# A two-layer vision tower on one core: expert outputs stored from ScalarE's queue and read back by tiles, and the last window's values made early

## What is computed

```python
# layer 0, experts: 64 experts n, each fed one weighted mean of the tokens of an image
d = softmax(logits, axis=tokens); c = softmax(logits, axis=experts)
xs = einsum('bmd,bmn->bnd', xn, d)
h  = gelu(einsum('bnd,ndh->bnh', xs, w1) + b1)
ys = einsum('bnh,nhd->bnd', h, w2) + b2
y  = einsum('bnd,bmn->bmd', ys, c)              # back to the tokens: "combine"
# layer 1, attention over a 5 x 5 window of the (image, token) grid, 4 heads of 24
xs = gelu(x @ fc1 + convB(convA(x @ fc1)))
q, k, v = split(xs @ qkv_w.T + qkv_b)
out = softmax(q . k[window] + bias) @ v[window]
x + (out @ proj_w.T + proj_b) @ fc2_w.T + fc2_b
```

## Time and profile before

| | us |
|---|---|
| median of 3 runs | 970.0 (961.99 to 974.12) |
| the profiled execution | 967.93 |
| its span, first to last instruction | 965.4 |
| expert loop, PE's first to last product | 266.1 to 440.7 |
| combine products | 461.7 to 478.2 |
| neighbourhood attention, with its preparation | 478.7 to 671.0 |

### The profile page before, as it was taken

The page is one execution under the profiler, slowest core; times in us unless marked ns, Lnnn a source line. Parts: engine busy times, 40 slices in busy tenths (PEclk is TensorE's granted clock), DMA queues, the critical chain, the costliest instruction groups (busy, mean ns, idle before and its releaser), DMA issues.

```text
span 965.4 us, 17426 instructions
## 1 busy us (share of the span) xinstructions
PE 839.8 (87%) x6089; PEld 601.3 (62%) x6089; DVE 443.0 (46%) x1486; ACT 317.8 (33%) x906; POOL 306.0 (32%) x267
## 2 busy tenths in 40 slices
PE   6889999899999999884898899994357999999991
PEld 6778888676556665543864577773344666666661
DVE  5764655558633322222635478863871222222220
ACT  2543333226533332223033377762001212122110
POOL 1440000000000000000125254541947588888444
PEclk9999999999989999997899599996556999999996
DMA  8994000090059999995130000000224355544222
GB/s 249 259 297 187 1 2 1 1 391 2 2 204 422 421 420 421 421 380 147 43 137 0 1 2 1 0 2 1 57 78 116 81 106 105 105 93 103 39 25 24
DMA packets 59881, 129.03 MB, mean 134 GB/s; under 512 B 26334, under 2 KB 42256, under 8 KB 50112
## 3 DMA queue, kind: packets, MB, share of 16 engines
q1 hardware_dynamic: 29858, 118.72, 34.2%
q0 software_dynamic: 29952, 9.36, 7.1%
HBM read 115.87 MB, written 11.49 MB: 132 GB/s over the span
## 4 chain that ended last, share of the span: by engine, by line
PE 72%; DMA 12%; DVE 5%; issue 4%; ACT 2%; SPq 2%; POOL 2%; DVEq 0%; POOLq 0%; ACTq 0%
PE bank L1929 9%; PE bank L1943 6%; PE bank L1934 5%; PE bank L1213 4%; DMA w1l<-in_w_dram 4%; PE bank L1611 3%; DMA xT<-in_xT_dram 3%; PE bank L1187 3%; PE bank L849 3%; PE bank L877 3%; DMA w1s<-in_w_dram 2%; PE bank L810 2%; PE bank L1637 2%; PE bank L1191 2%; PE bank L857 2%
## 5 line engine op out<-in xcount | busy, mean ns | idle before, releaser
L1305 POOL MEMSET xg<- 96x74 f32 x1 | 0.2, 158 | 405.9 <-PE bank L1269 405.9
L1865 POOL DMA_INDIRECT out_dram<-yr,put x48 | 105.8, 2203 | 58.2 <-issue 46.8
L1929 PE MATMUL bank<-zTa,w 128*128 128x372 f32 x256 | 90.3, 497 | 0.8 <-DVE zTb L2003 0.8
L2012 DVE TENSOR_TENSOR hT<-sg,bank 128x372 f32<-128x372 f32 x64 | 31.8, 538 | 107.7 <-ACT sg L1973 66.3
L1852 POOL DMA_INDIRECT zr<-z_rows,take x48 | 66.7, 1389 | 27.1 <-issue 26.8
L1929 PEld LDWEIGHTS bank<-zTa,w 128*128 128x128 f32 x256 | 47.5, 194 | 38.2 <-ACT sg L1973 8.4
L1153 DVE COPY eh<-bank 128x384 f32<-128x384 f32 x32 | 17.9, 558 | 111.5 <-PE bank L1191 111.5
L1943 PE MATMUL bank<-w2r,hT 128*124 128x192 f32 x384 | 66.1, 329 | 0.8 <-DVE hT L2012 0.8
L1973 ACT ACTIVATE sg<-bank 128x372 f32<-128x372 f32 x64 | 27.3, 478 | 115.6 <-PE bank L1934 115.6
L1943 PEld LDWEIGHTS bank<-w2r,hT 128*124 128x124 f32 x384 | 61.9, 187 | 3.9 <-issue 3.9
L1346 POOL TENSOR_TENSOR nl<-nl,nr 111x1036 f32<-111x1036 f32 x22 | 42.1, 1914 | 60.3 <-DVE nr L1463 60.3
(11 more groups left out here) (311 smaller groups left out, 1757.8 us busy)
## 6 DMA issues: line engine op xcount, KB each, us to landing
w1l<-in_w_dram SPq DMA_DIRECT2D x20, 1152.0 KB, 16.0
w2l<-in_w_dram SPq DMA_DIRECT2D x20, 1152.0 KB, 16.8
w1s<-in_w_dram SPq DMA_DIRECT2D x12, 1152.0 KB, 14.9
w2s<-in_w_dram SPq DMA_DIRECT2D x12, 1152.0 KB, 15.0
w<-in_w_dram SPq DMA_DIRECT2D x8, 1024.0 KB, 7.8
xt<-in_x_dram SPq DMA_DIRECT2D x22, 336.0 KB, 8.9
xT<-in_xT_dram SPq DMA_DIRECT2D x22, 333.0 KB, 8.1
w2r<-in_w2r_dram SPq DMA_DIRECT2D x8, 384.0 KB, 4.0
```

What stands on the lines that cost most here:

```text
L1865: nc.gpsimd.indirect_dma_start(rows_out, bass.IndirectOffsetOnAxis(ap=put[:, k:k + 1], axis=0), yr[e % 2][:, j, :], None, bounds_check=OUT ...
L1929: nc.tensor.matmul(bank[to + 2 * part + half][:, 0:HS], w13[b][:, 0, at:at + 128], zTa[b][:, half * HS:(half + 1) * HS], start=True, stop= ...
L2012: nc.vector.tensor_tensor(hT[:, m, half * HS:(half + 1) * HS], sg[half][:], bank[4 * (m % 2) + 2 + half][:, 0:HS], ALU.mult).then_inc(s_hT, 1)
```

## The change

There are two parts. First, all 32 pairs are stored to `ys`, by ACT: right behind its copy to `eo` it waits for that copy and issues the two stores on its own DMA queue. SP's loop only loads. When all stores have landed, SP reads everything back in four spans of images (0 to 5, 6 to 10, 11 to 15, 16 to 21), each with one read into all 128 partitions of `e1` and one into 64 of `e2`; `product(t)` waits for the span that holds t. Second, the three value tiles of the last window move to the first three turns of the attention loop, each with two of the unread products behind it.

```diff
@@ experts_sp
+            for s in range(NPAIR):
...
-                p = s - RING
-                if p >= 0:
-                    sp.wait_ge(s_do, p + 1)
-                    for e in range(2):
-                        n = p + e * NPAIR
-                        if p < DIRECT:
-                            sp.dma_start(ys_of[n], eo[b][e * B:(e + 1) * B]).then_inc(s_eoo[b], 16)
-                        else:
-                            for to, lo, hi in places(n):
-                                sp.dma_start(to, eo[b][e * B + lo:e * B + hi]).then_inc(s_eoo[b], 16)
...
+            sp.wait_ge(s_dy, FREED + 1)
+            sp.dma_start(e2[NE:2 * NE, 0:T], ins["b2"].rearrange("n (t d) -> n t d", d=ED)).then_inc(s_el, 16)
+            for b in range(EOB):
+                sp.wait_ge(s_eoo[b], rows_out_by(NPAIR - EOB + b))
+            pairs = ys_of[:, 0:2 * (T - 1)].rearrange("n (g t) d -> g n t d", g=2)
+            for k, (lo, hi) in enumerate(SPANS):
+                sp.dma_start(e1[:, lo:hi], pairs[:, :, lo:hi]).then_inc(s_rows[k], 16)
+                last = T if hi == T - 1 else hi
+                sp.dma_start(e2[0:NE, lo:last], ys_of[:, 2 * (T - 1) + lo:2 * (T - 1) + last]).then_inc(s_rows[k], 16)
@@ experts_act, output(p)
                 nc.scalar.copy(eo[p % EOB][:], bank[6 + b][:, 0:ED]).then_inc(s_do, 1)
+                act.wait_ge(s_do, p + 1)
+                for e in range(2):
+                    act.dma_start(ys_of[p + e * NPAIR], eo[p % EOB][e * B:(e + 1) * B]).then_inc(s_eoo[p % EOB], 16)
@@ combine_pe
-            pe.wait_ge(s_el, 16 * (1 + 2 * GB))
-            for b in range(EOB):
-                pe.wait_ge(s_eoo[b], rows_out_by(NPAIR - EOB + b))
+            pe.wait_ge(s_el, 16)
...
             def product(t):
+                k = [lo <= t < hi or t == hi == T - 1 for lo, hi in SPANS].index(True)
+                pe.wait_ge(s_rows[k], rows_in(k))
@@ value_tiles
-            if isinstance(t, int):
-                return [T + 1, T + 2, T + 3] if t == T - 1 else [t + 2]
-            return [t + 2]
+            return [] if isinstance(t, int) and t == T - 1 else [t + 5]
@@ near_pool
-            for j in range(2):
+            for j in range(5):
                 source(j)
@@ near_dve, spread(t)
-                if after(t, 3):
-                    dve.wait_ge(s_fV, t)
+                dve.wait_ge(s_fV, t + 3)
@@ near_pe, query(t)
-                if after(t, 4):
-                    pe.wait_ge(s_fVc, t - 1)
-                elif t == 0:
-                    pe.wait_ge(s_fVc, 2)
+                pe.wait_ge(s_fVc, t + 2)
...
+                if isinstance(t, int) and t < 3:
+                    value(t + 2, t % 2)
+                    dense_near(2)
```

More of the change, by code:

```diff
@@ L34 @@
 EOB = 4
-DIRECT = 27
+FREED = 27
+SPANS = ((0, 6), (6, 11), (11, 16), (16, 21))
 HALF_HID = HID // 2
@@ L453, in tower @@
         s_cxc = sem("expert_input_stored")
-        s_w1 = [sem(f"w1_in{q}") for q in range(RING)]
-        s_w2 = [sem(f"w2_in{q}") for q in range(RING)]
+        s_w1 = [sem(f"w1_slot_in{q}") for q in range(RING)]
+        s_w2 = [sem(f"w2_slot_in{q}") for q in range(RING)]
+        s_rows = [s_w1[2], s_w2[2], s_w1[3], s_w2[3]]
         s_dh = sem("expert_hidden_product")
@@ L1065, in dispatch_pe, with rows_in @@
             over_tiles(pe, [(1, logits), (0, transpose_x), (4, inputs), (3, transpose_d)], T, unroll=8)
+        def rows_in(k):
+            return 16 * len(range(2 + k // 2, NPAIR, RING)) + 32
         def experts_sp(sp):
-            for s in range(NPAIR + RING):
+            for s in range(NPAIR):
                 q = s % RING
[L1072 to L1080, removed]
-                p = s - RING
-                if p >= 0:
-                    b = p % EOB
-                    sp.wait_ge(s_do, p + 1)
-                    for e in range(2):
-                        n = p + e * NPAIR
-                        if p < DIRECT:
-                            sp.dma_start(ys_of[n], eo[b][e * B:(e + 1) * B]).then_inc(s_eoo[b], 16)
-                        else:
-                            for to, lo, hi in places(n):
-                                sp.dma_start(to, eo[b][e * B + lo:e * B + hi]).then_inc(s_eoo[b], 16)
[L1092 to L1102, removed]
@@ L1104, in places @@
-        def places(n):
-            return ((e1[n:n + 1, 0:T - 1], 0, T - 1), (e1[NE + n:NE + n + 1, 0:T - 1], T - 1, 2 * (T - 1)), (e2[n:n + 1, 0:T], 2 * (T - 1), B))
+                if s == EARLY:
+                    sp.wait_ge(s_h, 2 * T)
+                if s >= RING:
+                    sp.wait_ge(s_dh, s - RING + 1)
+                sp.dma_start(w1s[q][:], ins["w1"][s]).then_inc(s_w1[q], 16)
+                if s >= RING:
+                    sp.wait_ge(s_dy, s - RING + 1)
+                sp.dma_start(w2s[q][:], ins["w2"][s]).then_inc(s_w2[q], 16)
@@ L1107, in rows_out_by @@
         def rows_out_by(p):
-            return sum(16 * (2 if r < DIRECT else 2 * GB) for r in range(p % EOB, p + 1, EOB))
+            return 32 * (p // EOB + 1)
         def experts_act(act):
@@ L1275, in value_columns @@
         def value_columns(j):
-            return j * TP if not isinstance(j, int) or j <= T else (B - WIN + PADR) * S + (j - T - 1) * TP
+            if isinstance(j, int) and j < 2:
+                return j * TP
+            if isinstance(j, int) and j < 5:
+                return (B - WIN + PADR) * S + (j - 2) * TP
+            return (j - 3) * TP
         def value_tiles(t):
-            if isinstance(t, int):
-                return [T + 1, T + 2, T + 3] if t == T - 1 else [t + 2]
-            return [t + 2]
+            return [] if isinstance(t, int) and t == T - 1 else [t + 5]
         def router_columns(c):
@@ L1337, in sources @@
             def sources(t, q):
-                source.b = q % 2
+                source.b = (q + 1) % 2
                 for j in value_tiles(t):
@@ L1435, in values, with last_values @@
                     dve.wait_ge(s_nA, t - 1)
-                for i, j in enumerate(value_tiles(t)):
-                    value(j, vl[i] if isinstance(t, int) and t == T - 1 else vn[(q + 2) % 4])
+                for j in value_tiles(t):
+                    value(j, vn[(q + 2) % 4])
+            def last_values(t, q):
+                if isinstance(t, int) and t < 3:
+                    value(t + 2, vl[t])
             for j in range(2):
@@ L1479, in residual @@
                 nc.vector.bn_stats(hst[:, t, :], h[:, t, :]).then_inc(s_hst, 1)
-            over_tiles(dve, [(4, copy_w), (2, reciprocal), (1, logits), (3, values), (0, spread), (5, residual)], T, unroll=4, tail=2)
+            over_tiles(dve, [(4, copy_w), (2, reciprocal), (1, logits), (3, values), (0, spread), (0, last_values), (5, residual)], T, unroll=4, tail=2)
         def near_act2(act):
@@ L1599, in values @@
                 for j in value_tiles(t):
-                    value(j, (j if isinstance(j, int) else q) % 2)
+                    value(j, (q + 1) % 2)
             for j in range(2):
@@ L1629, in values_out @@
                 tiles = vl if isinstance(t, int) and t == T - 1 else [vn[(q + i) % 4] for i in range(3)]
-                pe.wait_ge(s_fVc, VT if isinstance(t, int) and t == T - 1 else t + 3)
+                pe.wait_ge(s_fVc, VT if isinstance(t, int) and t == T - 1 else t + 6)
                 if after(t, 1):
```

## The result

The changed kernel takes 983.15 us (977.39 to 985.98, four runs) where before took 966.88 (961.99 to 974.12) in the same comparison: a ratio of 1.0162, 95% interval 1.0118 to 1.0206. The forecast was 982, from +11.9 us on the profiled execution; measured are +15.2 us between the two profiled executions (967.93 and 983.08) and +16.3 between the medians. That 982 is nearer to 983.15 than 11.9 is to 16.3 is luck: it comes from the median of before, 970.0 in the three runs shown then and 966.9 here.

The account below looks back on a forecast made before the run. The prediction saw the late way of the outputs into e1 and e2 as bounding the experts' end, 21 us before the combine. Terms +19.3, +2 and -9.4 on 967.93 gave 979.8, median 2.1 higher: 982 us, range 960 to 1000.

Parts of the forecast that it names:

- The number of engines: Read into e1: outermost counts 2 and 128 allow only two DMA engines, so the e1 data take 41.3 us.
- Their rate: Read into e1: each of the two engines moves 25 GB/s, with 18.4 as the other end.
- rival (b): Read-back: each of the two engines moves less, 18.4 GB/s, giving 998 us; chance 0.12.
- The read-back: Between experts and combine: the last span lands near 491.5 and the combine ends near 497.5, +19.3 us.
- the waits between the groups: Combine: products come in four groups with PE waits of about 10 us, each ended by a read.
- Stores on ACT: Expert loop: two stores per pair on ACT, 0.6 us each, stay hidden in 3.35 us free per pair.
- Rival (c): Expert loop: ACT is held by its issues at 3 us each, giving 1009 us; chance 0.04.
- The values at the start: First three attention turns: an added value and two unread products each cost +2 us, between -2 and +6.
- two of 1.49 / 6: First three attention turns: two unread products, at twice the time, take 0.5 us each; 5.0 us in all with the values.
- At the end: Attention loop's end: last values_out starts 7.0 us earlier, 2.4 more from the clock; -9.4 us, between -7 and -10.
- Rival (a): Read-back: the read uses 16 engines, the combine ends near 466.1, time 950.5 us; chance 0.14.
- The one in (d): Attention loop: the values' early products cost what the end gives, 989 us; forecast together with this has 0.70.

Follow-up runs that it names:

- 64 rows: The changed kernel with each span's read into e1 made as two reads of 64 rows, one for each third of the images; 949.29 us.
- experts outermost: The changed kernel with the two outer dimensions of the e1 reads' source exchanged, experts (64) outside, thirds (2) inside, combine weights reordered to match; 952.45 us.
- part 1 alone: The kernel before with only the stores on ACT and the reading back by spans; 985.41 us, ratio 1.0177.
- part 2 alone: The kernel before with only the last window's values made in the first three attention turns; 962.83 us, ratio 0.9943.
- rows_62: The kernel with two reads of 64 rows per span, but each 64 rows read as 62 and 2; 982.92 us, ratio 1.0171.

## Why the prediction was right, and where its terms were off

**The number of engines** was the step that decided, and it was right: 0.13 x 16 = 2, shown by the trace's packets and by three runs in which that number changes while the bytes stay (64 rows, experts outermost, 62 rows). One of its reasons was weaker than it looked: the pieces have one partition as their destination, but behind it the same count of 21 or 22 rows as the source (1x21x192), so they couldn't tell which side sets the number. The changed kernel's read, 2 against 128, and the run with experts outermost, 64 against 128, can. **Their rate** was taken at 25 GB/s and measured at 26; the other end, 18.4, did not come, so rival (b) fell. **The read-back** is +19.3 us as forecast, by two errors that cancel: the last store landed at 442.9 and not 444.4, since a store lands 1.99 us from its issue and not 3.1, and from the first read's issue to the last landing it took 48.3 us and not 47.1. That it comes out to a tenth is luck: counted from the last `eo` copy the combine ends 20 us later in the changed kernel and 21 with part 1 alone. The bounds of the last store, 443.9 to 448.5, were off as well: issues of 0.45 and 3.05 us give 444.2 to 446.8. And the waits between the groups were announced as about 10 us, where the prediction's own sum left some 4; 10 us is the distance of the spans.

**Stores on ACT** stayed hidden: 0.56 us each in the median, PE 50.00 of 50 us busy, 161.9 us from the first `eo` copy to the last where it was 161.6, and moving them back to SP changed nothing that the runs can tell. Rival (c) fell: the longest issue was 1.78 us.

**The values at the start** were mis-sized: the first four turns took 3.5 us more in the changed kernel's trace, forecast +2 and within its bounds. The step "two of 1.49 / 6" misread its row: six records are three products, so a group of two takes 1.97 us and not 1.0, and the three turns add 8 us of PE's time and not 5. The scores give some of it back at a higher clock (1.26 us for four records, and 0.65 in the mean of the four turns in place of 0.50); the prediction took the clock as unchanged and allowed for this in the bound only. In other executions of the same code the four turns cost +0.7. **At the end** the term was -9.4 and is -8.1 (119.4 to 111.3). The wait went as forecast: from values_out of tile 19 to that of tile 20 it is 3.8 us in place of 10.7, -6.8 for the -7.0. From there to the last row statistics it is 6.9 in place of 8.7, -1.8 for the -2.4: the products run at clock 1.00 up to 682, but PE waits 1.07 us for ACT before the fc2 product at 681.15 (0.82 before), and the last fc2 product takes 1.05 us at clock 0.50 in both. The turns ahead are 0.6 us longer, for which the sum had no term. **The rest**, after the loop, is 1.2 us longer, for which the sum had no term; kernels that are alike there show 293.9 to 296.7, so it isn't the change's. +19.3, +3.5 and -8.1 with this 1.2 make the 15.9 by which the span grew.

**Rival (a)**, 16 engines, gave 950.5 by its sum, and the kernel that has them takes 949.3. Its size was right for partly wrong reasons: it let 0.88 MB land in 2.1 us at 420 GB/s, but at 233 it takes 3.8, and the four spans some 14 us. That is still under the 16.1 us of products, which run while the later spans come in, and the stores had landed earlier than the rival assumed. **The one in (d)** didn't come: part 2 alone is faster.

## What to carry to other kernels

Before a transfer is made larger, look at what stands outermost on both its sides: a leading dimension of 2, or 62 rows in place of 64, confined it to two of 16 engines and cost 30 to 34 us of 950, and exchanging two dimensions gave them back. Split a late read into pieces that its consumers wait for one by one: that was worth 13 us, most of it by the order of waits, since the rate differed little (203 to 215 GB/s in one span, 232 to 233 in four). Traces of like code differed by 3 us in the four turns in which PE's granted clock is between its two levels in the mean (19.7 us at 0.76, 22.5 at 0.65), so a price read from one such stretch needs the other as its bound.

## What the runs showed of the hardware

Sixteen engines that write into 64 partitions at a time moved 223 to 233 GB/s here, 203 to 215 with rows of 16 KB, and are shown busy all the while (share 1.04, 0.97 to 1.02 with the long rows); into 128 partitions they moved 394. So the share doesn't tell whether engines move data at their full rate, and the GB/s beside it does. By the Trainium skill, "SBUF — State Buffer", section "Door 1: The DMA port swizzle (why `[64,N]` ≈ `[32,N]`)", partitions 0 to 63 reach only 8 of 16 ports, for some 218 GB/s; the measured rates lie from 7% below to 7% above that figure. The prediction's first rival used 420 GB/s for these reads and didn't weigh this.

SP's issues of single reads took 9.53, 10.34 and 9.97 us in the changed kernel and up to 5.22 in rows_62, where two engines work off the earlier reads; with 16 engines at work the longest was 1.73. That SP is held until earlier reads have drained is the likely reason; it is not shown, as no run tried it. Nothing waited behind it here; loads queued behind such an issue would have gone out that much later.
